# Four moves of side work and a new instruction order in a two-layer attention and feed-forward kernel

## The chip, the cores and the metric

The kernel runs on one core of a Trainium2 chip. The metric is the device time of one execution in microseconds (us), as the median of several runs. A core has a matrix engine (TensorE, PE in the profile, whose weight loads are shown apart as PEld), a vector engine (VectorE, DVE), a scalar engine (ScalarE, ACT), a general engine (GpSimd, POOL) and SyncE (SP), which here issues most of the data transfers. Every engine works through its own list of instructions in order, and waits at a semaphore where an instruction says so.

## The reference, cut to what matters

64 sequences `x` of 128 rows by 128 columns, each with 77 context rows of 256 columns, go through two layers, each an attention-like part and a feed-forward part with a layer norm ahead and a residual sum behind:

```
# layer 0, attention (a_...): 8 heads of 16 columns, keys and values are the two halves of ctx
Q = heads(layernorm(x)) * 16**-0.5 ;  K, V = heads(ctx[..., :128]), heads(ctx[..., 128:])
x = x + softmax(Q @ K.T + b - 1e30 * (1 - mask)) @ V
# layer 0, feed-forward (b_...): weights are signs made of booleans, w = where(k, 1, -1)
h = concat(z, -z), z = layernorm(x) ; h = 2*relu(s0 * h @ w0) ; h = 2*relu(s1 * h @ w1) ; x = x + s2 * h @ w2
# layer 1, mixing (c_...): a projection, and a decaying sum over context patches picked by position
x = x + (rmsnorm(layernorm(x)) @ W_in + b_in) + depool(normalised ctx patches, patch_lens)
# layer 1, experts (d_..., e_...): 8 experts, the two best by gate, weighed by softmax probability
y = layernorm(x); p = softmax(y @ Wg.T + bg); w = p where in the top two, else 0
x = x + sum_e w[e] * (y @ W[e].T + b[e])
```

## The kernel before, in words

**Groups and stages.** The 64 sequences are worked through in 16 groups of four, g[0] to g[15]; a group's tile is 128 by 512. Parts a, b, c, d and e of different groups run at the same time: in the steady stretch, while group n is in the feed-forward layers (`b_layer`), group n+2 is in attention and group n-2 in the experts. For each engine the whole order is written out by hand as a long list of calls (`a_scores(g[3], 0)`, `b_low(g[1], 5)`, ...), and each call waits on semaphores for its inputs and for a free buffer. Nothing reorders it at run time.

**Part a.** `a_stats` (VectorE) takes mean and variance, `rstd` (GpSimd) makes `rs` and `nm` of them, the power in four small instructions; `normalise` (ScalarE, line 1549) writes `xn`, one instruction for each of four sequences. `a_turn_keys` and `a_turn_rows` (TensorE) transpose, `a_keys` and `a_queries` (ScalarE) copy out. `a_scores(g, 0)` and `(g, 1)` make scores of two sequences each, from which `a_highest` (VectorE) takes row maxima; `a_split_maxima` splits them in three bfloat16 parts (lines 927 to 933), `a_turn_maxima` transposes them, and `a_weights(g, q)` makes the scores again, transposed and less their maxima. `a_exponent(g, q)` (ScalarE, line 1604) takes the exponential, `a_values` multiplies with the values, `a_out_copy`, `a_turn_out`, `a_weigh` and `a_residual` bring the result back and add it.

**Part b.** `b_normalise` and `b_turns(g)` (transposes into PSUM banks 4 and 5) begin it. Then come eight `b_layer` calls and `b_last`; each result is split in a high half (`b_high`, ScalarE) and a low half (`b_low`, VectorE, line 969), since the matmuls are in float16. `b_residual` ends it. For group 0 the banks of `b_turns` are held before by attention of group 1 (`pa(g)` is banks 4 to 7 there): it waits for `a_exponent(g[1], 1)`.

**Parts c to e.** `c_turns`, `c_project`, `c_residual`; `d_turns`, `d_gate_scores`, `d_gates`, `d_gate_exp`, `d_top` make the gate weights `wgt`. `e_experts(g, j)` makes the eight experts' outputs of sequence j in two PSUM banks, `e_weigh` (VectorE, line 1046) multiplies them with `wgt` into one of two `weighed` buffers, `e_add` (GpSimd) halves them three times (1024 to 512, 256, 128 columns) and `e_out` adds the residual. For the last two groups `e_add` and `e_out` of j = 1 and 3 are on VectorE (lines 1056 to 1066).

**The head.** SyncE issues the loads in the order rows g[0], masks, rows g[1], keys g[0], mask rows, keys g[1], weights. ScalarE issues the loads of the booleans and scales. Constants that are made once:

- `make_weights` (ScalarE, lines 1532 to 1534): the three sign matrices, 512, 2048 and 512 columns, between the two `a_exponent` calls of g[0];
- `turn_weights` (TensorE, ten transposes) and `take_weights` (four ScalarE copies): the expert, input and gate weights, ahead of `a_values(g[0])`;
- `mark_ends` (VectorE), `count_ends` (TensorE, 64 small matmuls), `take_counts`, a trip through DRAM (`order_counts`), and `make_plug` (VectorE): the patch positions. SyncE's queue stands at `plugs_out` until `make_plug` is done, and the later loads stand behind it.

`keep_busy(n, bank)` is n matmuls of 512 columns into a bank that nobody reads; before, there are 17 of them in five places near the end.

## Time and profile before

| what | value |
|---|---|
| median of 3 runs | 539.12 us (539.06 to 539.27) |
| the profiled execution's own time | 538.97 us |
| its span, first to last instruction | 537.2 us |
| mean granted TensorE clock | 0.982 |
| busy: PE | 497.7 us (93%) |
| busy: DVE | 433.1 us (81%) |
| busy: ACT | 356.7 us (66%) |
| busy: POOL | 364.5 us (68%) |

The span plus 1.77 us outside it is the execution's time. An engine's busy time is the union of its instructions' times; "idle before" is what an engine stood still for ahead of an instruction, with the one that released it.

### The profile page before, as it was taken

Reading aid. Unit: us, or ns where it says so; the run is one execution under the profiler, and the core shown is the slowest. Engines: PE = TensorE matmul, PEld = TensorE weight load, DVE = VectorE, ACT = ScalarE, POOL = GpSimd, SP = SyncE. Lnnn points to the kernel's source line nnn. Section 1 sums busy time; section 2 is a strip of 40 time slices with the busy share of each in tenths; the row PEclk is TensorE's granted clock in tenths of the full one; section 3 lists DMA queues with packets and bytes.
Section 4 is the critical chain, followed back from the end, with each engine's and each line's share of the span. In section 5 each row is a group of like instructions: output and inputs, shape, how many; then the busy total and the mean of one; then the engine's idle time right before and its main releaser. Section 6 shows DMA issues by size and latency. Waiting matters only on the chain.

```text
span 537.2 us, 15110 instructions
## 1 busy us (share of the span) xinstructions
PE 497.7 (93%) x5549; PEld 324.0 (60%) x5549; DVE 433.1 (81%) x1404; ACT 356.7 (66%) x761; POOL 364.5 (68%) x633
## 2 busy tenths in 40 slices
PE   1756999999999999999999999999999999999893
PEld 1645565666656565766666566666666666655551
DVE  4735868899897979888897979799887785867897
ACT  3398698887967867677686866777566665655410
POOL 7644444588858869686868778686845857654865
PEclk9987899999999999999999999999999999999997
DMA  7402101010310101010110101000000000100010
GB/s 170 101 4 55 32 16 56 2 51 6 82 36 18 34 22 51 23 50 21 31 43 21 52 1 51 21 21 27 3 21 1 2 22 1 33 1 21 1 31 29
DMA packets 28503, 16.98 MB, mean 32 GB/s; under 512 B 3687, under 2 KB 28429, under 8 KB 28430
## 3 DMA queue, kind: packets, MB, share of 16 engines
q1 hardware_dynamic: 26670, 15.57, 10.5%
q8 instruction: 44, 0.72, 0.5%
q10 hardware_dynamic: 1760, 0.46, 0.4%
q14 instruction: 29, 0.24, 0.1%
HBM read 11.74 MB, written 4.24 MB: 30 GB/s over the span
## 4 chain that ended last, share of the span: by engine, by line
PE 64%; DVE 5%; issue 1%; ACT 0%; DVEq 0%
PE ps L2186 16%; PE ps L2134 16%; PE ps L2145 4%; PE ps L2079 4%; PE ps L2022 4%; PE ps L2096 4%; PE ps L2127 4%; PE ps L2164 2%; PE ps L2165 2%; PE ps L2104 2%; PE ps L2054 2%; PE ps L2177 2%; DVE weighed L1046 1%; PE ps L2083 1%; PE ps L2047 1%
## 5 line engine op out<-in xcount | busy, mean ns | idle before, releaser
L2186 PE MATMUL ps<-w_moeT,y4T 128*128 128x512 f32 x256 | 123.5, 607 | 1.2 <-DVE gd L1005 1.1
L613 POOL TENSOR_TENSOR sum<-weighed 128x512 f32<-128x512 f32 x60 | 76.1, 1269 | 71.2 <-DVE weighed L1046 71.2
L2134 PE MATMUL ps<-h,w 128*128 128x512 f16 x512 | 118.6, 379 | 0.0
L1638 ACT ACTIVATE h<-ps 128x512 f16<-128x512 f32 x128 | 74.1, 591 | 46.9 <-PE ps L2134 35.9
L1046 DVE TENSOR_TENSOR weighed<-ps,wgt 128x1024 f32<-128x1024 f32 x64 | 77.8, 1218 | 31.7 <-PE ps L2186 30.7
L969 DVE SCALAR_TENSOR_TENSOR h<-ps,h 128x512 f16<-128x512 f32 x128 | 85.6, 682 | 20.2 <-ACT h L1638 20.1
L2134 PEld LDWEIGHTS ps<-h,w 128*128 128x128 f16 x512 | 48.3, 98 | 56.2 <-issue 5.6
L1604 ACT ACTIVATE prT<-ps,maskT 77x1024 f32<-77x1024 f32 x64 | 67.3, 1101 | 14.8 <-PE ps L2083 14.5
L2186 PEld LDWEIGHTS ps<-w_moeT,y4T 128*128 128x128 f32 x256 | 45.1, 189 | 43.0 <-issue 35.0
L565 POOL TENSOR_TENSOR rs<-ve,neg_half 128x4 f32<-128x4 f32 x64 | 64.9, 1013 | 8.7
L560 POOL TENSOR_TENSOR ve<-mv,eps 128x4 f32<-128x4 f32 x64 | 14.2, 222 | 60.6 <-DVE mv L903 60.4
L615 POOL TENSOR_TENSOR sum<-sum 128x256 f32<-128x256 f32 x60 | 49.0, 817 | 4.7
L917 DVE TENSOR_REDUCE mx<-ps 128x8 f32<-128x616 f32 x64 | 47.7, 786 | 4.4 <-PE ps L2054 4.4
L2079 PE MATMUL ps<-qT,kT 32*77 32x128 f32 x1024 | 44.3, 288 | 2.6 <-ACT prT L1604 1.6
L2022 PE MATMUL ps<-ident,xn 128*128 128x128 f32 x256 | 40.5, 284 | 2.8 <-ACT xn L1549 2.5
L2022 PEld LDWEIGHTS ps<-ident,xn 128*128 128x128 f32 x256 | 30.6, 146 | 14.4 <-issue 8.1
L2127 PE MATMUL ps<-zT,w 128*128 128x512 f16 x128 | 37.1, 395 | 1.0 <-DVE zT L966 0.9
L2079 PEld LDWEIGHTS ps<-qT,kT 32*77 32x77 f32 x1024 | 31.0, 149 | 7.3 <-issue 3.6
L1549 ACT ACTIVATE xn<-xd,nm,rs 128x128 f32<-128x128 f32 x64 | 26.3, 482 | 13.0 <-POOL nm L567 13.0
L2096 PE MATMUL ps<-prT,vx 77*32 77x128 f32 x1024 | 31.3, 274 | 3.5 <-issue 3.0
L2145 PEld LDWEIGHTS ps<-w,h 128*128 128x128 f16 x512 | 29.6, 98 | 7.6 <-issue 5.7
L2096 PEld LDWEIGHTS ps<-prT,vx 77*32 77x32 f32 x1024 | 27.1, 110 | 10.2 <-issue 9.5
(171 smaller groups left out, 986.1 us busy)
## 6 DMA issues: line engine op xcount, KB each, us to landing
cx<-in_ctx SPq DMA_DIRECT2D x16, 308.0 KB
xa<-in_x SPq DMA_DIRECT2D x16, 256.0 KB, 3.0
out_x<-xo SPq DMA_DIRECT2D x16, 256.0 KB, 2.3
plugs<-plug_d SPq DMA_DIRECT2D x16, 77.0 KB
nat<-in_L_ffn_W SPq DMA_DIRECT2D x1, 512.0 KB
k_u<-in_L_ffn_k ACTq DMA_DIRECT2D x1, 256.0 KB, 3.9
k_u<-in_L_ffn_k ACTq DMA_DIRECT2D x1, 128.0 KB, 3.4
k_u<-in_L_ffn_k ACTq DMA_DIRECT2D x1, 64.0 KB, 4.6
```

Of the source, the lines that this page charges most:

```text
L565: nc.gpsimd.tensor_tensor(rs[n][:, p], ve[n][:, p], neg_half[:], ALU.pow).then_inc(ln.rs.sem, 1)
L613: nc.gpsimd.tensor_tensor(sum4[:], both[:, 0:4 * D], both[:, 4 * D:8 * D], ALU.add).then_inc(c_sum4.sem, 1)
L969: last = nc.vector.scalar_tensor_tensor(h[:, 1, (k - 1) % FC, :], src, 0.0, h[:, 0, (k - 1) % FC, :], ALU.max, ALU.subtract)
L1046: nc.vector.tensor_tensor(weighed[:, j % 2, :].rearrange("p (e d) -> p e d", e=E), pm(g, j).rearrange("p b (e d) -> p (b e) d", d=D), wgt[ ...
L1604: last = nc.scalar.activation(prT[:, 2 * q + j].rearrange("k (r e) s -> k r (e s)", r=R), pa(g)[0:NK, :, j * HR * S:(j + 1) * HR * S], ACT ...
L1638: last = nc.scalar.activation(h[:, 0, (k - 1) % FC, :], src, ACT.Relu)
L2022: last = pe.transpose(dst[:, j * rows:(j + 1) * rows], src(j), ident[0:rows, 0:rows])
L2079: pe.matmul(pa(g)[0:NK, r, at:at + S], kT[rows, g.p, e, b, :], qT[rows, g.p, b * S:(b + 1) * S], start=True, stop=False)
L2096: last = pe.matmul(pa(g)[32 * i:32 * i + 32, at // 4, (at % 4) * S:(at % 4 + 1) * S], vx[:, g.p, j, h, :], prT[:, j, h, :], start=True, st ...
L2127: last = pe.matmul(pb(g, k), w1[:, c * 128:(c + 1) * 128], zT[:, part, :], start=(part == 0), stop=(part == 1))
L2134: last = pe.matmul(pb(g, k), w2[:, i, c * 128:(c + 1) * 128], h1[:, g.p, part, i, :], start=(i == 0 and part == 0), stop=(i == FC - 1 and ...
L2186: last = pe.matmul(pm(g, j)[:, half, :], y4T[:, g.p, j * S:(j + 1) * S], w_moeT[:, half * 512:(half + 1) * 512], start=True, stop=True)
```

## The change

The last steps of two groups, work at the head, and the order of all five lists are changed.

1. **Sums at the end.** `how(g)` says who sums each sequence: for g[14] GpSimd, VectorE, GpSimd, VectorE; for g[15] GpSimd, ScalarE, VectorE, VectorE. VectorE no longer weighs into a buffer and adds in halves; it runs eight dependent instructions per sequence straight from PSUM, each `xo = psum[e] * wgt[e] + so far`. ScalarE's sequence is weighed in eight instructions (`e_weigh`), summed by nine TensorE matmuls (`e_sum`) and copied out (`e_take`).
2. **Norms shared.** For g[15] in parts c and d ScalarE normalises two sequences and VectorE two (`normalise_rest`). In part a, groups 1 to 3 are normalised by VectorE (`a_normalise`), and these use `rs` directly, not `nm`.
3. **Signs.** `make_weights` goes from ScalarE to VectorE. `turn_weights` and `take_weights` are cut in three pieces, later in the order, the copies on VectorE.
4. **Nineteen `keep_busy` matmuls** ahead of the first scores: 9 before `a_turn_keys(g[0])`, then 3, 4 and 3. Those at the end become 8 instead of 17, and they take `ones_bf` as data.
5. **Order.** The keys of g[0] are loaded before the rows of g[1]; `make_head_scale` comes first on VectorE; `turn_mask` comes ahead of the first scores and waits for `mark_ends`; ScalarE takes `a_keys(g[0])` before `a_normalise(g[0])`; `make_plug` comes right behind `make_halves`; rows of g[3] are loaded behind the plug. Groups 0 to 5 and 12 to 15 are reordered widely, the middle ones in a few places.

```diff
+        def how(g):
+            return {NG - 2: ("gpsimd", "vector", "gpsimd", "vector"), NG - 1: ("gpsimd", "scalar", "vector", "vector")}.get(g.n, ("gpsimd",) * G)
...
+            def make_weights():
+                dve.wait_ge(made_s, 6)
+                dve.wait_ge(made_halves, 1)
+                nc.vector.tensor_scalar(w1[:], k0_d[:], s_sgn[:, 7:8], None, ALU.mult)
+                nc.vector.tensor_scalar(w2[:], k1_u[:], s_sgn[:, 5:6], s_sgn[:, 6:7], ALU.mult, ALU.add)
+                nc.vector.tensor_scalar(w3[:], k2_u[:], 2.0, -1.0, ALU.mult, ALU.add).then_inc(made_ffn, 1)
...
+            def a_normalise(g):
+                dve.wait_ge(ln_a.rs.sem, ln_a.rs.of(g))
...
+                for j in range(G):
+                    last = nc.vector.tensor_scalar(xn[0][:, g.p, j * D:(j + 1) * D], xa[:, g.f, j * D:(j + 1) * D],
+                                                   mv[0][:, g.p, j, 0:1], rs[0][:, g.p, j:j + 1], ALU.subtract, ALU.mult)
...
+            def e_accumulate(g, j, half):
...
+                for e in range(4 * half, 4 * half + 4):
+                    so_far = xo if e else xd
+                    if e:
+                        dve.wait_ge(v_step.sem, v_steps(g, j) + e)
+                    last = nc.vector.scalar_tensor_tensor(xo[:, g.p, cols], pm(g, j)[:, e // 4, (e % 4) * D:(e % 4 + 1) * D],
+                                                          wgt[:, g.p, j, e:e + 1], so_far[:, g.p, cols], ALU.mult, ALU.add)
...
 # the head of VectorE's list
+            make_head_scale()
             a_stats(g[0])
             make_masks()
-            make_head_scale()
+            mark_ends()
             a_stats(g[1])
-            mark_ends()
+            take_mask()
             a_highest(g[0], 0)
+            a_normalise(g[1])
             take_counts()
-            make_halves()
             a_highest(g[0], 1)
             a_split_maxima(g[0])
-            take_mask()
+            make_halves()
+            make_plug()
             a_highest(g[1], 0)
+            a_stats(g[2])
             a_highest(g[1], 1)
-            a_stats(g[2])
-            a_stats(g[3])
             a_split_maxima(g[1])
+            a_normalise(g[2])
+            make_weights()
             a_weigh(g[0])
             a_residual(g[0])
             b_stats(g[0])
...
 # the head of ScalarE's list, after
+            a_keys(g[0]); a_normalise(g[0]); a_queries(g[0]); a_squares(g[0]); a_maxima(g[0]); a_queries(g[1]); a_keys(g[1])
+            a_exponent(g[0], 0); a_exponent(g[0], 1); a_squares(g[1]); a_out_copy(g[0]); a_maxima(g[1]); a_queries(g[2])
+            a_squares(g[2]); a_keys(g[2]); a_exponent(g[1], 0); b_normalise(g[0]); a_exponent(g[1], 1); b_high(g[0], 0)
...
 # the head of TensorE's list
+            keep_busy(9, 4)
             a_turn_keys(g[0])
+            keep_busy(3, 4)
             turn_ends()
+            keep_busy(4, 4)
             a_turn_rows(g[0])
+            turn_mask((s_ends, g[0]))
+            keep_busy(3, 4)
             a_scores(g[0], 0)
-            count_ends((s_ends, g[0]))
+            count_ends((s_mask, g[0]))
             a_scores(g[0], 1, (a_max[0], g[0]))
...
 # the end of VectorE's list
-            e_weigh(g[15], 1)
-            e_add(g[15], 1)
-            e_weigh(g[15], 2)
-            e_out(g[15], 1)
-            e_weigh(g[15], 3)
-            e_add(g[15], 3)
-            e_out(g[15], 3)
+            e_accumulate(g[15], 2, 0)
+            e_accumulate(g[15], 2, 1)
+            e_accumulate(g[15], 3, 0)
+            e_accumulate(g[15], 3, 1)
```

(The lists of ScalarE are written several calls to a line here; the file has one call a line.)

## Rows read from the trace of the kernel before

**Rows 1.** Windows by stage: us, busy (x instructions) by engine, PEclk, DMA share, GB/s.

```profile
0.00:10.85 10.85, 0.00 (x0) 0.03 (x1) 4.50 (x35) 3.14 (x6) 7.37 (x29) 1.00 0.67 155
10.85:26.70 15.85, 12.12 (x191) 10.01 (x195) 11.87 (x19) 6.37 (x19) 11.62 (x21) 1.00 0.55 124
26.70:50.08 23.38, 14.23 (x308) 12.23 (x296) 10.91 (x41) 22.82 (x48) 13.21 (x25) 0.85 0.02 5
...
50.08:90.00 39.92, 36.54 (x448) 23.40 (x449) 30.52 (x96) 30.96 (x69) 15.58 (x33) 0.91 0.18 52
...
90.00:500.00 410.00, 407.74 (x4488) 263.59 (x4486) 343.58 (x1124) 287.02 (x606) 291.12 (x489) 1.00 0.09 25
```

**Rows 2.** Windows of two stretches with PEclk 0.50, same columns.

```profile
36.90:43.30 6.40, 5.27 (x63) 4.75 (x64) 0.00 (x0) 6.25 (x18) 5.96 (x13) 0.50 0.02 4
...
50.75:57.10 6.35, 5.62 (x26) 2.82 (x29) 3.29 (x9) 4.29 (x9) 0.00 (x0) 0.50 0.38 102
```

**Rows 3.** Timeline of TensorE at the head: start, us, engine, line, tiles, [idle before].

```profile
10.85 0.75 PE L2022 MATMUL ps<-ident,cx 77*128 77x77 f32 x4 [10.85 <-DMA cx<-in_ctx]
...
25.80 0.66 PE L2079 MATMUL ps<-qT,kT 32*77 32x128 f32 x8
...
29.47 0.41 PE L2079 MATMUL ps<-qT,kT 32*77 32x128 f32 x8
30.45 1.10 PE L2008 MATMUL ps<-ident,weighed 128*128 128x128 f32 x8
...
50.08 0.74 PE L2022 MATMUL ps<-ident,xn 128*128 128x128 f32 x4 [0.77 <-ACT xn L1549]
```

**Rows 4.** Timeline of VectorE, GpSimd and SyncE at the head.

```profile
12.02 0.22 DVE L867 CAST ends_i<-ps 77x64 int32<-77x64 f32 x1 [3.53 <-PE ps L2002]
...
14.34 0.68 DVE L876 TENSOR_TENSOR within<-ends_f,expert 77x512 bf16<-77x512 f32 x1
...
20.45 1.90 POOL L524 TENSOR_TENSOR weighed<-nat 128x1024 f32<-128x1024 f32 x1
20.52 1.86 DVE L931 CAST mxb<-mr 128x32 bf16<-128x32 f32 x1
...
32.27 0.18 DVE L931 CAST mxb<-mr 128x32 bf16<-128x32 f32 x1
...
43.30 0.36 DVE L946 RECIPROCAL rden<-ps 128x32 f32<-128x32 f32 x1 [9.90 <-PE ps L2104]
...
47.02 0.46 SPq L416 DMA_DIRECT2D plug_d<-plug  x1
```

**Rows 5.** Timeline of ScalarE, 28 to 50 us.

```profile
28.98 0.71 ACT L1532 ACTIVATE w<-sum,s_sgn 128x512 f16<-128x512 f32 x1
...
32.19 2.10 ACT L1604 ACTIVATE prT<-ps,maskT 77x1024 f32<-77x1024 f32 x2
...
48.28 1.65 ACT L1549 ACTIVATE xn<-xb,nm,rs 128x128 f32<-128x128 f32 x4
```

**Rows 6.** Groups by line and shape on VectorE: count, busy, mean ns, idle before.

```profile
L969 DVE SCALAR_TENSOR_TENSOR h<-ps,h 128x512 f16<-128x512 f32 x128 | 85.6, 682 | 20.2 <-ACT h L1638 20.1
L1046 DVE TENSOR_TENSOR weighed<-ps,wgt 128x1024 f32<-128x1024 f32 x64 | 77.8, 1218 | 31.7 <-PE ps L2186 30.7 <-DVE wgt L1035 0.3 <-issue 0.2
...
L980 DVE SCALAR_TENSOR_TENSOR xc<-ps,s_sgn,xb 128x512 f32<-128x512 f32 x16 | 11.9, 744 | 2.0 <-PE ps L2145 2.0
```

**Rows 7.** Timeline of the last 20 us.

```profile
518.79 0.63 PE L2022 MATMUL ps<-ident,xn 128*128 128x128 f32 x4 [0.24 <-ACT xn L1549]
...
521.73 7.03 PE L2186 MATMUL ps<-w_moeT,y4T 128*128 128x512 f32 x16
...
524.83 2.36 DVE L1046 TENSOR_TENSOR weighed<-ps,wgt 128x1024 f32<-128x1024 f32 x2
...
530.53 1.21 DVE L1046 TENSOR_TENSOR weighed<-ps,wgt 128x1024 f32<-128x1024 f32 x1
...
533.83 0.50 DVE L1066 TENSOR_TENSOR xo<-oT,xd 128x128 f32<-128x128 f32 x1
```

More of the change, by code:

```diff
@@ L1216, in _ @@
             b_residual(g[4])
+            a_picks(g[5])
             b_low(g[5], 0)
@@ L1442, in _ @@
             d_stats(g[12])
+            a_weigh(g[14])
+            b_low(g[13], 5)
+            a_residual(g[14])
+            e_weigh(g[11], 3)
+            b_low(g[13], 6)
             b_stats(g[14])
-            e_weigh(g[11], 3)
-            b_low(g[13], 5)
-            b_low(g[13], 6)
+            a_picks(g[14])
             b_low(g[13], 7)
@@ new lines, in _ @@
+            b_high(g[6], 3)
+            c_turned(g[5])
+            b_high(g[6], 4)
+            a_queries(g[9])
+            a_maxima(g[8])
+            a_keys(g[9])
+            a_decays(g[8])
+            b_high(g[6], 5)
+            a_squares(g[11])
+            b_high(g[6], 6)
+            d_normalise(g[5])
+            b_normalise(g[7])
+            d_turned(g[5])
+            b_high(g[6], 7)
+            b_high(g[6], 8)
+            a_normalise(g[11])
+            d_gate_exp(g[5])
+            a_exponent(g[8], 0)
@@ new lines, in _ @@
+            b_high(g[7], 0)
+            a_exponent(g[8], 1)
+            b_high(g[7], 1)
+            b_high(g[7], 2)
+            a_out_copy(g[8])
+            c_normalise(g[6])
+            a_queries(g[10])
+            b_high(g[7], 3)
+            c_turned(g[6])
+            b_high(g[7], 4)
+            a_maxima(g[9])
+            a_keys(g[10])
+            a_decays(g[9])
+            b_high(g[7], 5)
+            a_squares(g[12])
+            b_high(g[7], 6)
+            d_normalise(g[6])
+            b_normalise(g[8])
```

864 lines of the change are left out of this document (479 added, 385 removed).

## The prediction

> **What bounds the kernel now.** I read first the windows by stage [rows 1], since the busy share of the whole span hides where TensorE stands still. From 90 to 500 us it is busy for 407.74 of 410.00 us: there TensorE sets the time, and no order of the other engines can give more than the 2.26 us that are left. The rest of its idle time is at the ends: 10.85 us before the first matmul, 3.73 us up to 26.70, 9.15 us from there to 50.08, and 3.38 us up to 90. At the other end stand the 8.4 us from the last matmul (521.73 + 7.03 = 528.76, [rows 7]) to the span's end at 537.2.
>
> Second, the clock. Two stretches of 6.40 and 6.35 us stand at a granted clock of 0.50, which is 1.2 of 2.4 GHz, with TensorE busy for 5.27 and 5.62 us of them [rows 2]. A third isn't in that column: the eight matmuls of line 2079 take 0.66 us at 25.80 and 0.41 us at 29.47 [rows 3], so up to 26.7 us the engine ran at the lower level although the column reads 1.00.
>
> Third, the timelines of the head. From 26.70 to 50.08 ScalarE is busy for 22.82 of 23.38 us [rows 1], while VectorE stands still for 9.90 us on end waiting for the attention result of g[0] [rows 4]. ScalarE bounds this stretch, and b_turns(g[0]), which opens the feed-forward work, waits for it at 50.08 [rows 3]. Behind it TensorE is over 90% busy, so a microsecond gained at b_turns is nearly one gained at the end.
>
> The profiled execution took 538.97 us for a span of 537.2, thus 1.77 outside it; the median of the runs is 539.12. My sum is made against 538.97.
>
> **Before 26 us: little.** The first keys land at 10.85 [rows 3]. With 256 KB of rows no longer ahead of them I estimate 8 to 9 us. That is not the start of the scores: turn_mask now stands before them and waits for mark_ends, which waits for turn_ends behind the keys. mark_ends took from 12.02 to 15.02, 3.0 us [rows 4]. So 8.5 + 0.7 (turning keys) + 1.3 (three dummies of 512 columns at 1.2 GHz, 0.43 each) + 0.4 + 3.0 + 0.4 + up to 1.3 (three dummies) gives first scores at about 15, not earlier than before. What follows gains elsewhere. The CAST of line 931 took 1.86 us at 20.52 and 0.18 us at 32.27 [rows 4]: the first began within 0.1 us of a GpSimd instruction of 1.90 us and ended with it. That instruction (the weights to turn) moves behind, which gives 1.7 us on the way to the maxima of g[0]. The nineteen matmuls stand in gaps where TensorE waits anyway, so I price them at nothing; without that cover ten of them (after the keys) cost 10 x 0.43 = 4.3 us at the lower clock, 2.2 at the upper. If they lift the clock by then, the matmuls up to 26.7 are shorter, but half of that stretch's steps are VectorE's and ScalarE's. I take 1.7 us, between 0 and 4.
>
> On SyncE's queue make_plug is the gate: it let the queue go only at 47.02 [rows 4]. Now it stands ahead of a_highest(g[1], 0), and what is queued behind it on VectorE waits for the trip of the counts through DRAM. The queue moves on some 20 us earlier; rows of g[3], put behind it, are wanted only about 37 us in. VectorE may lose 0 to 1.5 us; I count 1, in the walk below.
>
> **26 to 50 us: the main term.** Off ScalarE go make_weights (28.98 to 32.19, 3.2 us, just ahead of an exponential that TensorE and all of the rest wait for), four copies (line 1532 takes 0.71 us for 512 columns, so 1.6 at most for their 1160; I take 1.2) and the normalisations of g[2] and g[3] (1.65 each, as the one at 48.28) [rows 5]: 7.7 us out of an engine that is full. With the 1.7 from above b_turns could come 9.4 us earlier. Part of it comes back on VectorE. The matrices there: line 969 writes 512 columns in 0.68 us, line 1046 1024 in 1.22 [rows 6], so 0.15 us plus 1.05 ns a column, and 512 + 2048 + 512 columns make 3.7 us; bounds are half of it and, with waits on GpSimd, 5.5. They stand ahead of a_weigh(g[0]). Walking the new lists forward: the second exponential of g[0] ended at 34.29 [rows 5]; less 3.2 and 1.7, and 0.6 for a higher clock ahead of it, it ends near 28.8. With the 1 us for the plug, VectorE splits the maxima of g[1] and normalises g[2] up to about 31.3, make_weights runs to 35.0, by when the result of g[0] is back. a_weigh to b_normalise took 5.0 us (43.30 to 48.28, [rows 4, 5]): 40.0. b_normalise now stands ahead of a_exponent(g[1], 1): 1.65 and 2.10 us put the end of both at 43.75 and b_turns at 43.8, that is 6.3 us ahead of 50.08; the 3.1 us between this and 9.4 are VectorE's share and the handoffs. I take 6.3, bounds 3 and 9.4.
>
> A rule speaks against this part. Line 931 above shows VectorE standing as long as a GpSimd instruction runs. The Trainium skill, "SBUF — State Buffer" (section "SBUF: two separate sides"), says that the two share one port pair as an exclusive lock, which a VectorE instruction in a two-port mode must hold too; rows 4 agree. By it each of the new single-source instructions, twelve normalisations and three matrices, can wait for a whole GpSimd instruction and block the next. What that makes of the time is the second rival below.
>
> **50 to 90 us.** The ten weight transposes come back here: 1.10 us for eight [rows 3], 1.3 for all. VectorE gets the copies (1160 columns by the line above, about 1.7 us) and the normalisation of g[3] (four of 0.28, 1.1) on top of 30.52 of 39.92 us [rows 1]; it isn't full, and I charge a third, 0.9. The lower clock held from 50.75 to 57.10 with 5.62 us busy [rows 2]; in full this is worth 2.8. I take half, 1.4, since before b_turns the walk leaves TensorE idle often enough (between 35 and 43 us) to lose the clock again. The Trainium skill, "TensorE: Matmul & The Clock Gate" (section "What's actually happening"), says that the lower rate is the default and sustained work lifts it; by that rule the dummies up to 15 us don't guard this stretch. Sum: -1.3 - 0.9 + 1.4 = -0.8. The head is worth 6.3 - 0.8 = 5.5 us.
>
> **90 to 500 us: nothing.** 2.26 us of idle time bound the gain. The reordered calls touch mostly the groups near the ends. Loads of g[8] now stand behind store(g[1]); they have some 10 us in hand.
>
> **The tail.** A sequence on VectorE cost from 530.53 to 533.83 + 0.50, 3.8 us [rows 7]. Now eight dependent instructions of 128 columns: 0.15 + 0.13 by the line above; line 980 with a per-row scalar takes 0.74 against 0.68 of line 969 [rows 6], so 0.34, and 0.04 between them: 8 x 0.38 = 3.0 us. Bounds 2.2 (0.28 each) and 4.0 (0.50, line 1066). From the turn of the last gates' input, T = 518.79 [rows 7]: the first e_weigh began at 524.83, T + 6.0, and ends at T + 7.2. e_experts began at 521.73 and takes 1.76 us a sequence; it loses three dummies in front (0.65 us), so its third ends at T + 7.6. Two sums behind that: T + 7.8 + 6.0 = T + 13.8, and 2.9 for the store as now (537.2 - 534.33) gives T + 16.7, against 18.4: 1.7 us. ScalarE's sequence (eight instructions at 1.65 / 4 [rows 5], nine short matmuls behind the experts, a copy) I estimate to end near T + 13, hidden; if it took a microsecond more it would be the end. For T: halved normalisations save 0.8 us each, twice, but one e_weigh (1.2) and half a sum (1.5) now stand ahead of c_residual(g[15]), against one e_experts (1.8) that moved behind b_last. I give T 0.3. Tail 2.0 us, bounds -1 and 4.
>
> **Sum.** 538.97 - 5.5 - 2.0 = 531.47: 531.5 us, span about 529.7.
>
> **The rivals.**
>
> *The clock pays too* (527.0): it stays up from 15 to 90 us. Then the remaining 1.4 us of the second low stretch and half of 5.27, 2.6, of the first [rows 2] come on top, with 0.5 of steps before 26. For it: 19 matmuls, and ScalarE's handoffs come sooner. Against it: the idle pieces in my walk.
>
> *VectorE becomes the bound of the head* (535.5): port waits and make_weights at 5.5 us, b_turns gains 3 and the next stretch loses 1.5; 538.97 - 1.5 - 2.0. For it: rows 4, and 7.6 us of new work there (3.7, 1.7 and two normalisations). By the page of the Trainium skill named above each collision can cost as much as that of rows 4. Against it: 9.90 us of idle in one piece.
>
> *Slower* (540.5): a wait in the middle that comes back in each group. VectorE is busy 343.58 of 410 us there [rows 1]; if the new order or the earlier loads open one gap of 0.75 us for TensorE in each of the twelve groups between, 9 us are lost: 538.97 - 7.5 + 9 = 540.5. From 0.63 us a group it outweighs the 7.5. Against it: the lists of g[8] to g[11] hardly change.
>
> *The head's gain is not there* (538.9): the plug or the counts hold VectorE so long that b_turns gains under 1 us and the tail nothing.
>
> **How the numbers follow.** Forecast 0.50 (own range 528.5 to 534.5), clock 0.19, VectorE 0.19, slower 0.08, no change 0.04. The measurement tells 0.2%, 1.1 us, from no change. Faster 0.88, same 0.04, slower 0.08. The range 525.5 to 537.0 takes in the first three with the bounds of the main term and leaves out the last two.
>
> **What would show it.** Right: b_turns(g[0]) near 44 us; ScalarE no longer full before it, VectorE's long idle piece gone; first scores near 15 us and half-length matmuls before 20 us; 5 to 6 us of TensorE idle gone before 50; last sum some 3 us long per sequence; 90 to the end of the middle unchanged in length. Wrong: b_turns after 47 us, the sign matrices waiting long on VectorE, or idle time of TensorE in the middle above 3 us.

## The result and the profile after

The changed kernel took 540.69 us (median of 20 runs, 538.31 to 543.51); the kernel before, on the same chip, 539.20 (20 runs, 538.80 to 541.07). The ratio is 1.0026, 95% interval 1.0013 to 1.0038: slower by a quarter of a per cent, where 531.5 us was forecast. The execution profiled is one of the fastest: 538.32 us, span 536.3, against 538.97 and 537.2. So there are two questions: where the 6.8 us are that even this execution lacks (538.32 less 531.5), and why the typical one takes 2.4 us more.

The windows by stage, columns as in [rows 1] (the first two stretches are the same, the others differ from those by less than 0.1 us):

```profile
0.00:10.85 10.85, 6.45 (x23) 2.33 (x24) 4.90 (x31) 3.94 (x8) 7.47 (x28) 1.00 0.64 159
10.85:26.70 15.85, 10.44 (x189) 8.14 (x188) 11.63 (x30) 5.87 (x15) 8.20 (x22) 0.69 0.46 107
26.70:50.00 23.30, 16.41 (x297) 13.81 (x297) 18.99 (x56) 14.45 (x33) 17.22 (x28) 0.72 0.15 45
50.00:90.00 40.00, 36.28 (x466) 23.50 (x468) 30.16 (x95) 29.81 (x63) 10.14 (x27) 0.95 0.09 26
90.00:500.00 410.00, 407.80 (x4511) 264.76 (x4504) 348.20 (x1128) 288.99 (x613) 296.08 (x496) 1.00 0.09 26
```

In the third row the intended relief is there in full: ScalarE falls from 22.82 to 14.45 us and VectorE rises from 10.91 to 18.99. TensorE gained 2.2 us of busy time, in part because its matmuls were longer there: the half rate lasted up to 30.5 us, where the kernel before left it at 26.6.

The clock column (1.00 is 2.4 GHz, 0.50 is 1.2) has to be read with care. Up to the first rise of the clock it says 1.00 whatever the rate was. In the kernel before that rise came at 26.6 us, so the 1.00 of its second row in [rows 1] stands for half rate, as the prediction had found. The changed kernel rose at 6.6 us and fell back at 16.8, so its 0.69 is the higher clock of the two. The first sixteen score matmuls of each kernel show it, before and then after:

```profile
17.08 1.24 PE L2054 MATMUL ps<-kT,qT 32*128 32x154 f32 x16
```
```profile
13.05 0.69 PE L2220 MATMUL ps<-kT,qT 32*128 32x154 f32 x16
```

I follow the time by one event, ScalarE's first copy of the transposed input of part b, which opens part b of a group. In us, before and after: g[0] 50.85 and 47.75, g[1] 75.13 and 74.47, g[12] 399.49 and 397.78, the end 537.2 and 536.3. So 3.1 us won at g[0], 2.4 of them lost again by g[1], 1.1 won in the middle, 0.8 lost from g[12] to the end.

VectorE and then GpSimd of the changed kernel behind the first maxima (timelines: start, us, engine, line, operation, tiles, count):

```profile
13.82 1.51 DVE L994 TENSOR_REDUCE mx<-ps 128x8 f32<-128x616 f32 x2 [0.63 <-PE ps L2220]
15.24 3.11 DVE L983 TENSOR_SCALAR xn<-xa,mv,rs 128x128 f32<-128x128 f32 x4
18.28 0.67 DVE L947 TENSOR_SCALAR counts<-ps 16x512 f32<-16x512 f32 x1
```
```profile
15.15 1.00 POOL L639 TENSOR_TENSOR rk<-ssm,neg_half 77x4 f32<-77x4 f32 x1
16.12 0.18 POOL L628 TENSOR_TENSOR spare_pool<-spare_pool 1x1 f32<-1x1 f32 x1
16.25 0.60 POOL L629 COPY vx<-cx 77x512 f32<-77x512 f32 x1
16.80 0.51 POOL L568 MEMSET y3T<- 128x512 f32 x1
17.27 0.94 POOL L569 MEMSET y4T<- 128x1024 f32 x1
```

The normalisation of g[1], new on VectorE, takes 3.11 us for four steps that take 0.34 each at the least, and ends when GpSimd's unbroken row ends (17.27 + 0.94 = 18.21). Behind it stand the counts and the second half of the maxima. The timelines of TensorE and then of ScalarE, changed kernel:

```profile
19.00 0.78 PE L2188 MATMUL ps<-ident,cx 77*128 77x77 f32 x4 [2.78 <-DVE counts L947]
...
26.74 0.72 PE L2245 MATMUL ps<-qT,kT 32*77 32x128 f32 x8 [0.92 <-ACT prT L1684]
...
28.91 0.33 PE L2249 MATMUL ps<-mT,sel 24*77 24x128 bf16 x4
...
46.60 1.12 PE L2188 MATMUL ps<-ident,xn 128*128 128x128 f32 x4 [1.57 <-ACT prT L1684]
```
```profile
21.71 0.28 ACT L1674 ACTIVATE mT<-ps 128x128 bf16<-128x128 f32 x1 [8.15 <-PE ps L2229]
...
24.57 2.11 ACT L1684 ACTIVATE prT<-ps,maskT 77x1024 f32<-77x1024 f32 x2 [1.28 <-PE ps L2249]
29.27 2.11 ACT L1684 ACTIVATE prT<-ps,maskT 77x1024 f32<-77x1024 f32 x2 [2.59 <-PE ps L2249]
...
42.90 1.65 ACT L1629 ACTIVATE xn<-xb,nm,rs 128x128 f32<-128x128 f32 x4 [1.92 <-POOL nm L618]
44.45 2.09 ACT L1684 ACTIVATE prT<-ps,maskT 77x1024 f32<-77x1024 f32 x2
```

b_turns(g[0]) comes at 46.60 instead of 50.08 [rows 3]. ScalarE, which was to be the bound, has two long waits. The 8.15 us end with the copy of the maxima, at 21.71; in the kernel before it waited 2.34 and 3.04 us in the same part and made this copy at 23.56, so the changed kernel is ahead there. The 2.59 us stand between the two exponentials of g[0], and they are new. In them TensorE makes the second half of the transposed scores, `a_weights(g[0], 1)`, from 26.74 to 29.24 at half rate, and it starts only when the first exponential is done. In the kernel before it did the same from 29.13 to 30.52, while ScalarE was busy with make_weights up to the second exponential at 32.19. TensorE, kernel before:

```profile
29.13 0.46 PE L2079 MATMUL ps<-qT,kT 32*77 32x128 f32 x8 [1.56 <-ACT prT L1604]
...
30.28 0.24 PE L2083 MATMUL ps<-mT,sel 24*77 24x128 bf16 x4
```

The clock, by windows of the changed kernel laid on its stretches at 0.50 and on the gap of 512 us (columns as above):

```profile
16.80:30.50 13.70, 9.44 (x145) 8.03 (x145) 8.21 (x23) 4.92 (x8) 4.67 (x16) 0.50 0.20 50
...
33.90:37.30 3.40, 2.73 (x13) 2.47 (x13) 2.60 (x4) 2.09 (x8) 3.15 (x5) 0.50 0.01 2
44.10:54.40 10.30, 7.48 (x58) 4.42 (x51) 7.75 (x14) 5.92 (x11) 5.17 (x8) 0.50 0.00 0
512.20:515.00 2.80, 0.00 (x0) 0.00 (x0) 2.57 (x14) 0.00 (x0) 2.21 (x6) 1.00 0.00 0
515.20:518.60 3.40, 3.40 (x5) 1.15 (x6) 2.37 (x3) 0.88 (x2) 2.46 (x4) 0.50 0.00 0
```

27.4 us stand at 1.2 GHz in the first 90. In the kernel before the column has 13.6 (two stretches of 6.8), but its matmuls ran at half rate from the first one at 10.85 up to 26.6 as well, which makes 29 us. So the change moved the half rate in the head and did not add any. One stretch is new at the end, behind 2.8 us in which TensorE did nothing. There the timelines of TensorE and then of VectorE read:

```profile
510.20 1.98 PE L2356 MATMUL ps<-w_moeT,y4T 128*128 128x512 f32 x4 [0.57 <-DVE weighed L1121]
515.03 3.68 PE L2356 MATMUL ps<-w_moeT,y4T 128*128 128x512 f32 x4 [2.85 <-DVE xo L1139]
518.51 0.85 PE L2155 MATMUL ps<-ones_bf 128*128 128x512 bf16 x3
519.20 0.60 PE L2188 MATMUL ps<-ident,xn 128*128 128x128 f32 x4
```
```profile
511.48 0.68 DVE L1069 TENSOR_TENSOR xd<-ps,xc 128x512 f32<-128x512 f32 x1
...
527.43 0.35 DVE L1139 SCALAR_TENSOR_TENSOR xo<-ps,wgt,xd 128x128 f32<-128x128 f32 x1 [1.23 <-PE ps L2356]
527.82 2.67 DVE L1139 SCALAR_TENSOR_TENSOR xo<-ps,wgt,xo 128x128 f32<-128x128 f32 x7
```

A sequence is summed in 3.1 us, as priced. But the experts of (14,3) wait for the accumulate of (14,1), which c_residual and d_stats of g[15] cut in two, then run at half rate (3.68 us against 1.98), and the turn of d of g[15] (the prediction's T) stands behind them, at 519.20. Counted from the opening of g[12], T comes after 121.4 us instead of 119.3, so 2.1 us later and not 0.3 earlier. What follows T takes 17.1 us instead of 18.4.

### The profile page after: what moved, and what is told of

Read it like the earlier page. It is cut to its first block, busy times and chain, and to the rows that moved or that the text cites. A ratio compares the mean times of both kernels' runs of the same rounds, so it can differ in the third digit from the quotient of the medians.

```text
span 536.3 us, 15187 instructions
## 1 busy us (share of the span) xinstructions
PE 504.6 (94%) x5577; PEld 327.4 (61%) x5577; DVE 442.3 (82%) x1438; ACT 348.9 (65%) x747; POOL 357.9 (67%) x629
## 4 chain that ended last, share of the span: by engine, by line
PE 76%; DVE 12%; issue 2%; ACT 1%; DVEq 0%; ACTq 0%
PE ps L2300 20%; PE ps L2356 19%; PE ps L2245 5%; PE ps L2311 5%; PE ps L2188 5%; PE ps L2262 5%; PE ps L2293 4%; PE ps L2332 3%; PE ps L2220 2%; PE ps L2333 2%; PE ps L2270 2%; PE ps L2347 2%; DVE xo L1139 2%; DVE h L1046 1%; DVE weighed L1121 1%
## 5 line engine op out<-in xcount | busy, mean ns | idle before, releaser
L2356 PE MATMUL ps<-w_moeT,y4T 128*128 128x512 f32 x256 | 125.8, 617 | 4.5 <-DVE xo L1139 3.2
L1121 DVE TENSOR_TENSOR weighed<-ps,wgt 128x1024 f32<-128x1024 f32 x59 | 71.9, 1218 | 31.1 <-PE ps L2356 30.5
L1684 ACT ACTIVATE prT<-ps,maskT 77x1024 f32<-77x1024 f32 x64 | 67.3, 1101 | 16.9 <-PE ps L2249 16.8
L666 POOL TENSOR_TENSOR sum<-sum 128x256 f32<-128x256 f32 x59 | 46.3, 784 | 4.6
L2188 PEld LDWEIGHTS ps<-ident,xn 128*128 128x128 f32 x256 | 30.5, 146 | 15.5 <-issue 3.5
```

The source lines that it names most:

```text
L1121: nc.vector.tensor_tensor(weighed[:, place(g, j), :].rearrange("p (e d) -> p e d", e=E), pm(g, j).rearrange("p b (e d) -> p (b e) d", d=D) ...
L1684: last = nc.scalar.activation(prT[:, 2 * q + j].rearrange("k (r e) s -> k r (e s)", r=R), pa(g)[0:NK, :, j * HR * S:(j + 1) * HR * S], ACT ...
L2188: last = pe.transpose(dst[:, j * rows:(j + 1) * rows], src(j), ident[0:rows, 0:rows])
L2356: last = pe.matmul(pm(g, j)[:, half, :], y4T[:, g.p, j * S:(j + 1) * S], w_moeT[:, half * 512:(half + 1) * 512], start=True, stop=True)
```

## The experiments

But for two further profiles of the changed kernel, each was timed in 11 or 12 executions against 23 to 35 of the kernel before on its chip, whose median was 539.2 to 539.5 us; intervals are 95%.

**Which end of the kernel.** Both lists of calls reach the same state on every engine in the middle of group 8; there one can be put behind the other.

```diff
e_head:  changed kernel up to g[8]; order, sums and normalisations of before from there
e_tail:  kernel before up to g[8]; those of the changed kernel from there
```

> The changed kernel's order and functions up to the middle of group 8 (about 280 us), and from there the kernel before: its order, its alternate sums of groups 14 and 15 on VectorE, its normalisations of group 15 whole on ScalarE. What the head and the first groups bring is 1.7 us at g[8] in the two profiles. Theory A (the head keeps a small gain, and the tail has given it back): 537.0 to 538.0 us, some 1.7 us below before. Rival (the head's gain is eaten in the middle whatever the tail is, because ScalarE and VectorE had slack stored in their queues): within 0.5 us of before, 539. Rival (the head as changed costs time, by the clock that falls at 17 us): 540 or more.

> The kernel before up to the middle of group 8, and from there the changed kernel: its order, the accumulating steps on VectorE, the sum of (15,1) on TensorE and ScalarE, the shared normalisations of group 15. My prediction gave the tail 2.0 us. Theory A (the changed tail is no better, since the experts of (14,2) wait for the accumulate of (14,1) and the turn of d of group 15 behind them): 539 to 541 us, no gain. Rival (the tail gains its 2 us and the head loses them): 537 us.

e_head 540.41 us, 1.0027 (1.0003 to 1.0051); e_tail 539.82, 1.0001 (0.9975 to 1.0027). The kernel with the changed head alone has the whole loss. The changed tail alone shows neither gain nor loss; its interval reaches down to 1.3 us and leaves out the 2.0 us of the prediction. Theory A was wrong on the head, by its run times, and right on the tail.

**The nineteen matmuls.**

```diff
e_nodummy, against the changed kernel:
-            keep_busy(9, 4)
             a_turn_keys(g[0])
-            keep_busy(3, 4)
             turn_ends()
-            keep_busy(4, 4)
             a_turn_rows(g[0])
             turn_mask((s_ends, g[0]))
-            keep_busy(3, 4)
e_dummy:  the same four calls put into the kernel before
```

> The changed kernel without the nineteen matmuls ahead of the first scores; nothing else differs. Theory A (they raise the clock at 7 us, but TensorE then waits 2.8 us at 16 us and the clock falls again until 31 us, so they buy little): within 0.7 us of the changed kernel. Rival (they pay: the first turns and scores at half rate make the keys, rows and first scores some 1 to 2 us late): 1 to 2 us slower than the changed kernel. Rival (they bring the fall of the clock on, by using up what the chip grants early): 1 to 3 us faster than the changed kernel, with full rate in the profile beyond 17 us.

> The kernel before with the nineteen matmuls ahead of its first scores alone. Theory A (free, and worth what the clock gives between 7 and 17 us, bounded by waits on other engines): 0 to 1 us below before. Rival (they shift the stretches of half clock that the kernel before has at 37 and at 51 us into its first 30 us, where TensorE is hardly the bound, and gain 1 to 3 us). Rival (the fall of the clock comes with them, as in the changed kernel: 1 us or more slower).

e_nodummy 539.06 us, 1.0006 (0.9985 to 1.0026); e_dummy 538.79, 1.0001 (0.9979 to 1.0024). So 1.6 us between the two medians of the changed kernel, with ratios whose intervals overlap, and nothing on the kernel before.

The mean clock of a run moves clearly: its median is 0.966 to 0.972 in the five kernels with the four calls or the first of them that were timed (the changed one, e_head, e_dummy, and e_nine and e_clean_dummy below) and 0.980 to 0.988 in all that lack them. But this mean counts the time ahead of the first rise as full clock. The matmuls brought the first rise to between 6.6 and 12.1 us in the six profiles with all nineteen; in the fourteen others it came between 24.2 and 42.7. Counting the half rate from the first use of the keys up to 90 us, it held for 27 to 38 us with the nineteen and for 29 to 44 without. So they didn't bring more of it; they moved it. The first scores, at 1.24 us for sixteen matmuls without them, took 0.69 us in three of the six profiles, 1.06 in one, and 1.24 to 1.25 in two.

To see a typical execution I profiled the changed kernel twice more, unchanged:

> The changed kernel, unchanged, for a second profile. Theory A (its slower executions are those in which more half clock falls into the stretches where TensorE is the bound, from 44 us on): if the time is 540 us or more, the stretch of half clock that begins at 44 us is longer, or another lies behind it, and g[1]'s block b opens later than 74.5 us by as much as the time is above 538.3. Rival (a slower transfer or another engine): the same clock stretches, and the lost time elsewhere.

> The changed kernel, unchanged, for a third profile: as e_after_b.

540.56 and 541.20 us. From g[1] on they are the same as the first to 0.5 us; part b of g[1] opens at 76.72 and 77.84 us instead of 74.47. In e_after_b the lengths at 0.50 in the clock column are the same too, so my theory was wrong there and the rival right: the loss is made before 20 us. TensorE's timeline, the first profile and then e_after_b:

```profile
7.64 0.49 PE L2188 MATMUL ps<-ident,cx 77*128 77x77 f32 x4 [0.87 <-DMA cx<-in_ctx]
7.97 0.81 PE L2155 MATMUL ps<-ones_bf 128*128 128x512 bf16 x3
8.71 0.28 PE L2165 MATMUL ps<-ident,ends 64*77 64x64 f32 x1
8.92 1.04 PE L2155 MATMUL ps<-ones_bf 128*128 128x512 bf16 x4
```
```profile
8.31 0.77 PE L2188 MATMUL ps<-ident,cx 77*128 77x77 f32 x4 [1.47 <-DMA cx<-in_ctx]
8.87 1.49 PE L2155 MATMUL ps<-ones_bf 128*128 128x512 bf16 x3
10.29 0.39 PE L2165 MATMUL ps<-ident,ends 64*77 64x64 f32 x1
10.61 1.76 PE L2155 MATMUL ps<-ones_bf 128*128 128x512 bf16 x4
```

The keys land 0.67 us later. In the first execution the clock had risen by then, at 6.6 us; in this one it rose at 12.1, and the matmuls that nothing reads take 0.5 us each ahead of the turn of the ends: 8.71 becomes 10.29, and the counts come 2.0 us later. The cover under which the prediction priced them at nothing was gone (it had priced that case at 4.3 us for ten at the lower clock, 2.2 at the upper). In e_after_c the keys are as late, the clock rose at 7.6 us, ahead of them, the counts still come 1.7 us later than in the first, and the lower clock holds from 14.4 to 41.7 us. From the first use of the keys to the first matmul of the scores it took 5.1 to 5.2 us in the twelve profiles of the changed head that lack the ten, 5.3 to 5.7 in the four that have them and in which the clock had risen by then, and 6.6 in e_after_b. So the ten cost 0.2 to 0.6 us, and 1.5 when the clock is late. The Trainium skill, "TensorE: Matmul & The Clock Gate" (section "What's actually happening"), says that the point at which the rate rises varies from run to run of one kernel; these three agree, with 6.6, 12.1 and 7.6 us.

The ten were then taken away alone:

```diff
             keep_busy(9, 4)
             a_turn_keys(g[0])
-            keep_busy(3, 4)
             turn_ends()
-            keep_busy(4, 4)
             a_turn_rows(g[0])
             turn_mask((s_ends, g[0]))
-            keep_busy(3, 4)
```

> The changed kernel with the nine matmuls ahead of the first keys and without the ten that stand between the first turns and the first scores. In the changed kernel's profile of 538.3 us the keys had landed at 7.6 us and the ten ran at full rate; in that of 540.6 us the keys landed at 8.3 us, TensorE had stood idle for 1.47 us, and the ten ran at half rate, ahead of the turns of the ends and of the rows: the counts came at 20.3 us instead of 18.3. Theory A (the ten in the way of the first real steps cost the 1.6 us): about 539.0 us, as e_nodummy, with a clock nearer 0.98. Rival (the half clock from 14 or 17 us on costs it, and the nine alone bring it): clock 0.97 and 540.5 us.

539.68 us, 1.0004 (0.9982 to 1.0025), median clock 0.966. The time lies between the two theories and the clock is the rival's. Whether the nineteen cost the 1.6 us at all, and how that divides, isn't settled: each part is smaller than the intervals.

**Normalisations on VectorE.** In e_nodummy that of g[1] took 3.35 us, and ScalarE was idle for 8.15. e_norm1 gives it back to ScalarE, e_norm3 all three:

```diff
-                return ln.n == 0 and 1 <= g.n <= 3
+                return ln.n == 0 and 2 <= g.n <= 3        # e_norm1; in e_norm3 4 <= g.n <= 3, that is, never
vector:  -a_normalise(g[1])  -a_normalise(g[2])  -a_normalise(g[3])
scalar:  +a_normalise(g[1]) behind a_queries(g[0]), g[2] behind a_exponent(g[0], 1), g[3] behind a_exponent(g[1], 1)
```

> As e_nodummy, with the normalisation of group 1 back on ScalarE, behind the queries of group 0, where ScalarE is idle from 14.7 to 22.9 us; those of groups 2 and 3 stay on VectorE. In e_nodummy its four steps took 3.35 us on VectorE, between the two halves of the maxima of group 0. Theory A (VectorE's own chain is the bound of the first 23 us, and this stood on it): the counts come about 3 us earlier, at 16.5 us, the maxima copy on ScalarE at about 19.8 instead of 22.93, and g[0]'s block b (the copy that opens it, 48.5 us in e_nodummy) 2 to 3 us earlier; the end 1 to 3 us earlier, about 537. Rival (the next wait takes over, because keys and rows of group 1 and the first exponent pair wait for something else such as the plug or the masks): under 0.5 us at the end.

> As e_norm1, with the normalisations of groups 2 and 3 back on ScalarE too, so that none is on VectorE; make_weights stays on VectorE. Each is 1.65 us on ScalarE. My prediction said that taking them from ScalarE gives 1.65 us each at g[0]'s block b. Theory A (in the stretch 26 to 50 us ScalarE has idle time of its own now, so their place does not matter): within 0.5 us of e_norm1 at the opening of g[0]'s block b and at the end. Rival (my prediction's step): 1.5 to 3.3 us later than e_norm1.

e_norm1 539.27 us, 0.9994 (0.9978 to 1.0010); e_norm3 537.85, 0.9961 (0.9944 to 0.9977), the first that is clearly below the kernel before. Taking the three normalisations *off* ScalarE was a loss in the run time, which both theories had missed. The profile doesn't explain it: there g[0] opens 2.2 us later than in e_norm1, as the rival has it, and g[1] 0.9 later. But e_norm3's profile is of one of its slowest executions (539.44 us), e_norm1's of one of its fastest (537.54), and e_norm3_old below, which has e_norm3's head, opens g[0] at 48.30 and g[1] at 74.26 us, against 48.48 and 75.72 in e_norm1. So the rival's step isn't shown.

Of e_norm1 the profile shows why one alone does little. The counts come at 16.8 us as expected (19.5 in e_nodummy), but the maxima copy is not earlier, because the next VectorE instruction stands still in its place (VectorE, then GpSimd, of e_norm1):

```profile
20.49 2.17 DVE L1086 CAST mxb<-mr 128x32 bf16<-128x32 f32 x1
22.70 0.19 DVE L1088 TENSOR_TENSOR mxb<-mr,mxb 128x32 bf16<-128x32 f32 x1
```
```profile
20.67 0.60 POOL L644 COPY vx<-cx 77x512 f32<-77x512 f32 x1
21.21 0.51 POOL L583 MEMSET y3T<- 128x512 f32 x1
21.68 0.94 POOL L584 MEMSET y4T<- 128x1024 f32 x1
```

It ends at 22.66, GpSimd's last fill at 22.62. The prediction counted this cast's collision as removed, since the weights to turn had moved; the fills of ones had moved into their place.

**GpSimd alone.** The same kernels with two of GpSimd's calls moved and nothing else:

```diff
gpsimd:  make_ones() behind make_weights_to_turn(), a_values_in(g[1]) behind make_signs()
e_port:  in e_nodummy;  e_clean:  in e_norm3;  e_clean_dummy:  in e_norm3 with the nineteen matmuls
```

> As e_nodummy, with two calls moved on GpSimd alone: the two fills of ones (0.5 and 0.94 us) go behind the weights to turn (47 us), and the copy of group 1's values behind the signs. In e_nodummy the four steps of a_normalise of group 1 on VectorE (0.34 us each at the least) took 3.35 us while GpSimd ran exactly these. Theory A (while GpSimd works back to back on tiles, a normalisation or a cast on VectorE stands still until it is done): the four steps take 1.4 to 2.2 us, the counts come 1 to 2 us earlier than 19.5, and the maxima copy of group 0 on ScalarE 1 to 2 us earlier than 22.9. Rival (the steps are slow by themselves, or the long one waits for the reciprocal square root on GpSimd): 3.3 us again.

> As e_norm3 (no normalisation on VectorE, no nineteen matmuls), with the same two calls of GpSimd moved as in e_port. In e_norm3 one cast of 128x32 took 2.17 us at 20.6 us, beside the same fills, where 0.18 is its least. Theory A: the cast is back at 0.2 us, the maxima copy of group 0 is at 21.4 instead of 23.4, and g[0]'s block b opens 2 us earlier than in e_norm3; the end about 1.5 to 2 us earlier than e_norm3's 537.85 us median, 536. Rival (the fills, at 47 us now, hold VectorE there, and the gain goes): e_norm3's time within 0.5 us.

> As e_clean, with the nineteen matmuls of the changed kernel ahead of the first scores. Between the changed kernel and e_nodummy they made the granted clock of the whole run 0.971 against 0.984 and the time 1.6 us longer; on the kernel before they changed the time by 0. Theory A (they spend the early grant of full clock on nothing, and twice as many us at half clock follow in the first 60 us): clock about 0.97, and 0.5 to 2 us slower than e_clean. Rival (with VectorE out of the way TensorE's rate in the first 25 us counts, and they pay 0.5 to 1 us).

The row of e_port that settles the mechanism:

```profile
16.73 1.11 DVE L1061 TENSOR_SCALAR xn<-xa,mv,rs 128x128 f32<-128x128 f32 x4
```

1.11 us for the four steps instead of 3.35, with the same VectorE order and the same data: they had stood still for GpSimd. By the rule of the Trainium skill named in the prediction ("SBUF — State Buffer", the lock on the shared port pair) this is what should happen; the trace agrees that VectorE stands still, though for longer than one GpSimd instruction. In e_port part b of g[0] opens at 46.69 us (48.51 in e_nodummy); in e_clean at 46.32 (50.68 in e_norm3, 0.65 of it from later keys). The run times don't follow: e_port 539.91 us, 1.0007 (0.9990 to 1.0024); e_clean 538.66, 0.9985 (0.9975 to 0.9996); e_clean_dummy 538.99, 0.9985 (0.9971 to 0.9999). So e_port is no faster than e_nodummy and e_clean no faster than e_norm3: the collision is real in the traces, but its removal isn't seen in the run times, and Theory A of e_clean (536 us) failed. In the profiles g[1] opens at 75.12 in e_port against 75.68, so two thirds of the gain are gone by there. The half rate isn't the reason: from the first use of the keys up to 90 us it held for 34 us in both e_port and e_nodummy, 33 in e_clean and 38.5 in e_norm3. What takes the gain stays open. The nineteen matmuls cost nothing measurable on e_clean.

The pair e_port and e_clean differs in the three normalisations alone, as e_nodummy and e_norm3 do. Here putting them back on ScalarE is worth 0.22%, there 0.45%. In e_port they hardly stand still for GpSimd ahead of the maxima (1.11 us for the four steps), so that collision can't be all that they cost; the rest isn't shown.

**The weights' copy.** From g[0] to g[1] the changed kernel lost 2.4 us. TensorE waited there for VectorE:

```diff
vector:  take_weights(1) behind b_stats(g[1]) instead of ahead of a_weigh(g[1])
```

> As e_nodummy, with one call moved on VectorE: the copy of the second half of the expert weights (0.7 us) behind the weighing, residual and statistics of group 1 instead of ahead of them. In e_nodummy TensorE waited 1.8 us at 63 us for that weighing. Theory A (VectorE is the bound of the stretch 50 to 75 us, in which the changed kernel gave back 2.5 us of its lead): the wait shrinks by 0.7 us and g[1]'s block b opens 0.7 us earlier. Rival (the wait is elsewhere right after): no change at g[1]'s block b.

The waits of TensorE from 50 to 76 us, e_nodummy and then e_take:

```profile
PE ps L2378 <- DVE att L1103: 1.8, 1, 1.8
```
```profile
PE ps L2378 <- DVE att L1103: 0.7, 1, 0.7
```

The wait shrank as expected and g[0] to g[1] took 26.7 us instead of 27.2; the run time is 539.25 us, 0.9997 (0.9980 to 1.0014), so 0.5 us is too little to be seen in it.

**The tail.** First the order on VectorE, in e_nodummy:

```diff
vector:  e_weigh(g[14], 0)
-        e_accumulate(g[14], 1, 0)
         c_residual(g[15])
         d_stats(g[15])
+        e_accumulate(g[14], 1, 0)
         e_accumulate(g[14], 1, 1)
```

> As e_nodummy (the changed kernel without the nineteen matmuls), with one call moved on VectorE: the first four accumulating steps of (14,1) behind c_residual and d_stats of group 15 instead of ahead of them. In the changed kernel c_project of group 15 ended at 509.6 us and c_residual started at 511.48, behind an expert weighing and four steps of 0.38 us. Theory A (the split accumulate is what the tail lost): c_residual starts at about 510.1 where c_project ends at 509.6, everything up to the end follows 1.4 us earlier, and from the last b_last to the end it takes 37.7 us instead of 39.1. Rival (the experts of (14,3), which wait for the whole of that accumulate, come later instead and keep d_turns of group 15 where it was): no change, 39.1 us.

540.63 us, 1.0011 (0.9995 to 1.0026): the rival's case. c_residual comes 1.4 us sooner after its project, but the experts of (14,3) wait as long (3.00 us), and from g[12] to the end it is 138.6 us. Then the clock in that gap, in e_norm3, and the old end behind the same head:

```diff
             e_experts(g[14], 2, (c_weighed, g[14], 1))
+            keep_busy(12, 0, (c_yT, g[15]))
             e_experts(g[14], 3, (c_weighed, g[14], 2))
```

> As e_norm3, with twelve matmuls of 128x512 in bf16 that nothing reads on TensorE between the experts of (14,2) and of (14,3), where TensorE waited 2.85 us for VectorE. Theory A (the granted clock falls there because TensorE stood idle, and the experts of (14,3), which stand ahead of the turn of d of group 15, then take 3.3 to 3.7 us instead of 1.98): no half clock near 515 to 521 us, the experts of (14,3) take 2.0 us, and from the opening of g[12]'s block b to the end it takes 137.0 us instead of 137.8 to 138.6. The median about 1 us below e_norm3's 537.85. Rival (the fall follows something else): the half clock stays and the twelve cost up to 0.5 us.

> As e_norm3 up to the middle of group 8, and from there the order and the functions of the kernel before. Theory A (the old end takes 137.7 us from g[12]'s block b, the new one 138.1 on the average because of the half clock): 0.3 to 0.5 us below e_norm3 in the median, within what can be measured. Rival (the new end is worth my prediction's 2.0 us): 2 us above e_norm3.

The timeline of TensorE in e_tailwarm:

```profile
511.14 1.99 PE L2434 MATMUL ps<-w_moeT,y4T 128*128 128x512 f32 x4 [0.48 <-DVE weighed L1199]
512.97 2.75 PE L2233 MATMUL ps<-ones_bf 128*128 128x512 bf16 x12
515.97 1.98 PE L2434 MATMUL ps<-w_moeT,y4T 128*128 128x512 f32 x4 [0.26 <-DVE xo L1217]
```

The half clock is gone and the experts take 1.98 us. It was gone in e_combo below too, with the same twelve; without them it was gone in one profile of thirteen (e_norm1). From the opening of g[12] to the end it took 137.6 to 137.7 us with the old tail in five profiles, 137.9 to 138.6 with the new one in twelve that had the half clock, and 137.1 in the three that had not. So in the profiles the new tail is worth 0.6 us, and the half clock behind its gap takes that and 0.2 to 1.0 more. In the run time: e_tailwarm 537.74 us, 0.9970 (0.9957 to 0.9982), the same as e_norm3; e_norm3_old 538.75, 0.9992 (0.9982 to 1.0003), 0.9 us above e_norm3, where its profile says it should be slightly below. The changed kernel and e_head (1.0026 and 1.0027), which differ in the tail too, show no such step. What makes it here stays open.

**Together.** e_best is e_clean with e_take's move and the old tail; e_combo is e_tailwarm with e_take's move.

> As e_clean up to the middle of group 8, with the copy of the second half of the expert weights behind group 1's weighing as in e_take, and from there the order and the functions of the kernel before: its alternate sums on VectorE at the end. From the opening of g[12]'s block b to the end the old tail took 137.7 us in two profiles and the new one 138.1 to 138.6 in five. Theory A: 0.5 to 1 us below e_clean, near 535.5 us. Rival (the two tails are the same within what can be measured): e_clean's time.

> As e_tailwarm (537.74 us: the changed kernel without the nineteen matmuls, all normalisations of group 1 to 3 on ScalarE, twelve matmuls in the gap ahead of the experts of (14,3)), with the copy of the second half of the expert weights behind group 1's weighing as in e_take, where it cut the wait of 1.8 us ahead of layer 5 of group 0 to 0.7. Theory A: 0.5 to 1 us below e_tailwarm, near 537.0. Rival (the wait moves to the next read): the same as e_tailwarm within 0.3 us.

e_best 537.97 us, 0.9969 (0.9953 to 0.9986); e_combo 536.93, 0.9961 (0.9941 to 0.9981), the lowest median of all: 0.39% (2.1 us) below the kernel before by the ratios and 0.65% below the changed one, from putting back the three normalisations, leaving out the nineteen matmuls, one call moved and twelve matmuls in the tail's gap. e_norm3, which has the first two of these edits alone, has the same ratio, so the other two show no gain in the run time.

## Why the prediction was wrong

**The step that failed is the main term, "26 to 50 us", and in it the sentence that ScalarE bounds this stretch, so that what goes off it is gained.** It was full and did stand ahead of b_turns, and the relief came in full (8.4 us off ScalarE), but of 6.3 us at b_turns 3.5 came. The walk had the copy of the maxima of g[0] at 21.9 (23.56 less 1.7), and it came at 21.71. It had the second exponential of g[0] end at 28.8, having taken off the whole 3.2 us of make_weights, and it ended at 31.4. These 2.6 us are nearly all of the 2.8 missing; from there to b_turns it took 15.2 us, as in the walk (15.0). What stood in the place of make_weights was TensorE's a_weights(g[0], 1), which had been hidden behind it: ScalarE waits 2.59 us for it, so 0.6 of the 3.2 us were gained. The wait is there in every profile without make_weights between the two exponentials, 2.59 us where TensorE was at half rate (ten profiles) and 1.48 at full rate (seven); it is absent in the three profiles with it.

**A premise failed too: that "a microsecond gained at b_turns is nearly one gained at the end".** Of 3.1 us at g[0] 0.7 were left at g[1]; in e_clean 4.5 us at g[0] became 1.2. That VectorE bounds part of the stretch behind b_turns is shown by e_take's wait (1.8 to 0.7 us), but only half of that came at g[1], and the rest of the give-back stays open.

**The normalisations.** The walk charged that of g[2] and not that of g[1], which took 3.11 us on the way to the maxima. The 1.65 us each for those of g[2] and g[3] had the wrong sign in the run time: the three back on ScalarE are worth 0.45% in one pair and 0.22% in the other. make_weights was over-priced on VectorE, 2.1 us instead of 3.7 (34.43 to 36.49).

**"Before 26 us: little."** The first scores came at 12.91, not 15: the keys landed at 7.64 instead of 8.5, the matmuls in front ran at full rate, and mark_ends took 2.8 us. The 1.7 us for the cast of line 931 came in this execution (it took 0.18 us), but by luck of order: the normalisation had absorbed the collision, and without it (e_norm1) the cast had it back. Pricing the nineteen matmuls at nothing was 0.2 to 0.6 us short, and 1.5 in e_after_b.

**"50 to 90 us"**: -0.8 forecast, -2.4 measured up to g[1]. The transposes and copies cost about as said, but the copy stands ahead of the weighing of g[1] that TensorE waits for (1.8 us), and nothing of the lower clock was saved (+1.4 in the sum): 7.8 us of it stand behind b_turns instead of 6.8.

**"90 to 500 us: nothing"** gave 1.1 us, within its bound of 2.26: idle time of 1.26 us at g[3] fell to 0.3. The rival that slows by a gap in each middle group did not occur; that its 540.5 us is near the result is luck.

**The tail**: 2.0 forecast, -0.8 in the profile, nothing in e_tail. The sum's price was right (3.1 us for 3.0), and what follows T gained 1.35 us of the 1.7 forecast; T was not right, 2.1 us later instead of 0.3 earlier. The walk let c_residual pass but didn't follow the experts of (14,3) and the clock behind their wait. In e_norm1, where the half clock was absent, T is only half a microsecond late.

**The rivals.** "VectorE becomes the bound of the head" had the number at b_turns right (3 us) and more lost behind it (1.5; measured 2.4). Its mechanism is there in part: the port waits are, but make_weights never took the 5.5 us it set, and TensorE's a_weights isn't in it. Its 535.5 us missed because it kept the tail at 2.0. The 6.8 us that the profiled execution lacks are thus 3.2 at g[0] (3.1 for 6.3), 1.6 from there to g[1], 2.8 in the tail and nearly 0.3 outside the span (2.0 instead of 1.77), less the 1.1 of the middle.

**Why the typical execution is slower than before** is shown only as far as the head goes. The normalisations on VectorE have a share that two pairs show, 0.22 to 0.45%. The nineteen matmuls may have one (1.6 us between two medians, none in the two other pairs), and so may the landing of the first load. How the normalisations cost it isn't shown.

## What to carry to other kernels

Before taking work off a full engine, ask what the other engines do while it runs: relief counts only up to the second-latest chain, here TensorE's next matmuls (2.59 us where 3.2 us of work had been). Walk the receiving engine's chain too, with the neighbour on its port in view: a short cast or normalisation on VectorE can stand still for a whole row of GpSimd's work, though here its removal didn't show in the run time. A clock column that starts at 1.00 is checked against the length of one kind of matmul before two kernels are compared by it. Matmuls that only keep the clock up belong in waits that nothing real can cut short; ahead of a first load whose landing varies they end up in front of the work. Where the executions of one kernel spread by several us, use a profile for where time goes and the medians for how much, and take more than one profile of the changed kernel.

## What was not expected of the hardware

A VectorE instruction stood still not for one GpSimd instruction but through a row of them: in e_norm1 a cast that takes 0.18 us alone took 2.17, through a COPY and two MEMSETs (0.60, 0.51 and 0.94 us), and ended 0.04 us behind the last.

Matmuls that nothing reads, run early, moved the half rate instead of saving it: 27 to 38 us of it up to 90 us with nineteen, 29 to 44 without, counted from the first use of the keys. At the end, the full rate was kept in both profiles with twelve matmuls in a wait of 2.85 us, and in one of thirteen without. What decides between the two isn't shown by these runs.

The first load of the keys, issued at the same place, was first used between 7.64 and 8.99 us in sixteen profiles and at 10.62 in a seventeenth (e_combo). In the two later profiles of the changed kernel, with the keys 0.7 us later than in the first, g[1] opened 2.2 and 3.4 us later, while from g[1] to g[12] it took 323.3 us in all three: between these three the spread comes from the head, not from the steady state.
